# Attention scores by head pairs in a gated Flamingo layer with a mixture of experts, on one core

## What is computed

```python
def attn(ctx, latents, mask):               # latents = layernorm(x)
    xn, ln = layernorm(ctx), layernorm(latents)
    q  = ln @ Wq.T                          # 4 heads of 64
    kv = concat([xn @ Wkv.T, ln @ Wlkv.T])  # 64 + 1024 keys
    k, v = split(kv)
    qn, kn = rmsnorm(q) * SCALE, rmsnorm(k) # per head
    p = softmax(where(mask, qn @ kn.T, -max))
    return (p @ v) @ Wo.T + bo
x = x + tanh(g_xattn) * attn(ctx_768, layernorm(x), mask)
x = x + tanh(g_ffn) * top2_of_8_experts(layernorm(x))   # 256 -> 1024 -> 256
```

## Time and profile before

| | |
|---|---|
| runs, median | 1214.55 us (1213.91 to 1215.9, three runs) |
| profiled execution, span | 1218.7 us |
| PE busy | 1021.0 us (84%) |
| PEld busy | 828.1 us (68%) |
| DVE busy | 784.3 us (64%) |
| ACT busy | 688.7 us (57%) |
| POOL busy | 382.1 us (31%) |
| mean granted TensorE clock | 0.916 of full speed |

### The profile page before, as it was taken

One profiled execution on the slowest core, in us unless ns is written; L12 is line 12 of the kernel. 1 busy time (PEld: TensorE's weight loads), 2 busy tenths in 40 slices (PEclk: granted clock), 3 DMA queues, 4 the chain that ended last, 5 costly groups with the idle time before them and its releaser, 6 DMA issues. The chain is left out here.

```text
span 1218.7 us, 20071 instructions
## 1 busy us (share of the span) xinstructions
PE 1021.0 (84%) x5940; PEld 828.1 (68%) x5940; DVE 784.3 (64%) x1603; ACT 688.7 (57%) x1084; POOL 382.1 (31%) x275
## 2 busy tenths in 40 slices
PE   4689986699976798975898950799999999999992
PEld 4546565565665565654565650699999999999992
DVE  5946778666769565869574555366757575775751
ACT  4867758576848476848576811344544445463530
POOL 3510205316106234106242105134334343452321
PEclk9979999699989699999698975799999999999997
DMA  3010001101000100010110015324244242442325
GB/s 104 1 37 1 1 0 36 37 14 57 1 26 9 36 35 35 0 35 0 34 52 17 0 35 169 108 48 112 46 115 119 43 117 43 117 111 49 43 35 155
DMA packets 44964, 61.93 MB, mean 51 GB/s; under 512 B 7265, under 2 KB 38753, under 8 KB 44865
## 3 DMA queue, kind: packets, MB, share of 16 engines
q0 software_dynamic: 17520, 33.27, 12.2%
q1 hardware_dynamic: 27408, 28.29, 7.9%
HBM read 37.34 MB, written 28.39 MB: 54 GB/s over the span
## 5 line engine op out<-in xcount | busy, mean ns | idle before, releaser
L1500 PE MATMUL psH<-xT_hi,Q 128*128 128x256 f32 x1120 | 205.5, 282 | 10.8 <-DVE Q L1426 9.3
L1513 PE MATMUL psY<-K,g_hi 128*128 128x256 f32 x1120 | 203.3, 283 | 0.0
L1357 POOL DMA_INDIRECT total<-y_out,token_i x70 | 114.2, 1631 | 230.3 <-PE psH L1500 188.8
L1500 PEld LDWEIGHTS psH<-xT_hi,Q 128*128 128x128 f32 x1120 | 175.3, 190 | 12.5 <-issue 12.5
L1513 PEld LDWEIGHTS psY<-K,g_hi 128*128 128x128 f32 x1120 | 171.6, 188 | 0.0
L1500 PE MATMUL psH<-xT_lo,Q 128*128 128x256 f32 x560 | 157.6, 281 | 0.0
L1513 PE MATMUL psY<-K,g_lo 128*128 128x256 f32 x560 | 157.2, 281 | 0.0
L1390 ACT ACT_TABLE_LOAD x35 | 44.9, 1283 | 170.2 <-PE psH L1500 170.2
L1390 ACT ACTIVATE g<-psH,b_col 128x256 f32<-128x256 f32 x280 | 113.8, 473 | 30.6 <-DVE g_lo L1454 27.6
L630 ACT ACTIVATE p_ring_hi<-psS,shift 128x1024 fp32r<-128x1024 f32 x80 | 89.3, 1116 | 60.5 <-PE psS L1170 56.5
L472 POOL TENSOR_TENSOR rr<-ssm,minus_half 128x8 f32<-128x8 f32 (+1 forms) x36 | 60.0, 1666 | 194.5 <-DVE ssm L720 194.5
(11 more groups left out here) (226 smaller groups left out, 2182.9 us busy)
## 6 DMA issues: line engine op xcount, KB each, us to landing
lnf<-routed SPq DMA_DIRECT2D x35, 258.0 KB, 2.7
xr<-in_L_ffn_w POOLq DMA_DIRECT2D x7, 1024.0 KB
xn<-in_L_ffn_w POOLq DMA_DIRECT2D x7, 1024.0 KB
xr<-in_x SPq DMA_DIRECT2D x4, 1024.0 KB, 5.3
total<-xb SPq DMA_DIRECT2D x4, 1024.0 KB, 4.5
routed<-pad_rows SPq DMA_DIRECT2D x8, 258.0 KB
total<-y_out,token_i POOLq DMA_INDIRECT x70, 3.9
routed<-big,slot_i POOLq DMA_INDIRECT x64
```

Of the source, the lines that this page charges most:

```text
L1357: pool.indirect_dma_start(total, bass.IndirectOffsetOnAxis(ap=token_i[:, m:m + 1], axis=0), y_out[:, m, :], None, bounds_check=NTOK + TM - ...
L1500: ins = pe.matmul(o, l, r, start=(n == 0), stop=(n == len(parts) - 1))
L1513: ins = pe.matmul(psY[m][:, 0:D], l[:, c, cols], r[:, c, :], start=(c == 0 and n == 0), stop=(c == HC - 1 and n == 2))
```

## The change

A step of attention is no longer one head with 1024 queries but a pair of heads with 512 queries. Step index k = i // 9 now counts (pair, half of the queries); the 512 columns of the even head lie in the first PSUM bank of the buffer and those of the odd head in the second. The stacked tiles go: `q_hi`, `q_lo`, `k_hi`, `k_lo` hold each pair's even head on partitions 0 to 63 and its odd head on 64 to 127. The scores are three passes, each as two products of 64 rows, one on the lower row half and one on the upper. `heads_hi` has two instructions of 128 partitions for a tile, `heads_lo` two. V_lo of the context keys is read with all 128 rows (the upper 64 are zero). The denominators of a step now belong to two heads; their instructions keep their shapes. `attention_hi` waits for other counts, and for its last half pair it waits until all values are multiplied, since its target is one of the probability buffers. `attention_lo` of the first half stands ahead of the last denominators. The memset of K2's pad goes.

```diff
-            K2 = sb("K2", [P, H // 2, S + P], F32R)
...
+            PAIRS = H // 2
+            q_hi, q_lo = Q1[:, 0:PAIRS, :], Q1[:, PAIRS:H, :]
+            k_hi, k_lo = K1[:, 0:PAIRS, :], K1[:, PAIRS:H, :]
...
-                        for odd in range(2):
-                            keep, other = halves(odd)
-                            q_src, k_src, cols = turned_heads(t, keep)
-                            if t < T:
-                                act.activation(Q1[keep, odd:H:2, cols], q_src, ACT.Copy, scale=gqk[keep, 0:1])
-                            act.activation(K1[keep, odd:H:2, cols], k_src, ACT.Copy)
-                            ins = act.activation(K1[other, odd:H:2, cols], k_src, ACT.Copy)
-                        ins.then_inc(qk_hi_ready, 1)
+                        q_src, k_src, cols = turned_heads(t)
+                        if t < T:
+                            act.activation(q_hi[:, :, cols], q_src, ACT.Copy, scale=gqk[:, 0:1])
+                        act.activation(k_hi[:, :, cols], k_src, ACT.Copy).then_inc(qk_hi_ready, 1)
...
-                        act.wait_ge(o_read, b * 2 * H + (4 * c + 3 + n))
+                        act.wait_ge(o_read, b * 2 * H + (4 * c + 2 + 2 * n))
+                        if c == PAIRS - 1 and n == 0:
+                            act.wait_ge(av_done, b * NI + NI)
...
-                        for odd in range(2):
-                            keep, other = halves(odd)
-                            q_src, k_src, cols = turned_heads(t, keep)
-                            if t < T:
-                                dve.scalar_tensor_tensor(
-                                    out=Q1[other, odd:H:2, cols], in0=q_src, scalar=gqk[keep, 0:1],
-                                    in1=Q1[keep, odd:H:2, cols].bitcast(F32), op0=ALU.mult, op1=ALU.subtract)
-                            ins = dve.tensor_tensor(K2[keep, :, cols], k_src, K1[keep, odd:H:2, cols].bitcast(F32), ALU.subtract)
-                        ins.then_inc(qk_ready, 1)
+                        q_src, k_src, cols = turned_heads(t)
+                        if t < T:
+                            dve.scalar_tensor_tensor(out=q_lo[:, :, cols], in0=q_src, scalar=gqk[:, 0:1],
+                                                     in1=q_hi[:, :, cols].bitcast(F32), op0=ALU.mult, op1=ALU.subtract)
+                        dve.tensor_tensor(k_lo[:, :, cols], k_src, k_hi[:, :, cols].bitcast(F32), ALU.subtract).then_inc(qk_ready, 1)
...
                     denominators(H - 1, 0)
                     quotients(H - 1, 0)
+                    attention_lo(PAIRS - 1, 0)
                     denominators(H - 1, 1)
-                    attention_lo(H // 2 - 1, 0)
                     quotients(H - 1, 1)
-                    attention_lo(H // 2 - 1, 1)
+                    attention_lo(PAIRS - 1, 1)
...
-                        for n in range(2):
-                            pe.matmul(scores_psum(i)[:, n * HALF:(n + 1) * HALF], K1[:, h, keys], Q1[:, h, n * HALF:(n + 1) * HALF],
-                                      start=True, stop=False)
-                        rows_hi = slice(0, DH) if h % 2 == 0 else slice(DH, P)
-                        for n in range(2):
-                            ins = pe.matmul(scores_psum(i)[:, n * HALF:(n + 1) * HALF], K2[rows_hi, h // 2, keys],
-                                            Q1[rows_hi, h, n * HALF:(n + 1) * HALF], start=False, stop=True)
+                        keys, cols = slice(kt * P, (kt + 1) * P), slice(n * HALF, (n + 1) * HALF)
+                        products = ((k_hi, q_hi), (k_lo, q_hi), (k_hi, q_lo))
+                        for m, (kk, qq) in enumerate(products):
+                            for odd in range(2):
+                                rows_of = slice(odd * DH, (odd + 1) * DH)
+                                ins = pe.matmul(scores_psum(i)[:, odd * HALF:(odd + 1) * HALF], kk[rows_of, pair, keys],
+                                                qq[rows_of, pair, cols], start=(m == 0), stop=(m == len(products) - 1))
                         ins.then_inc(s_done, 1)
...
-                        vh, vl = V_hi[:, kt, v0:v0 + P], V_lo[0:p, kt, v0:v0 + P]
+                            vh, vl = V_hi[:, kt, v0:v0 + P], V_lo[:, kt, v0:v0 + P]
+                            products = [(vh, ph), (vh, pl), (vl, ph)] if kt < T else [(vh, ph), (vl, ph)]
```

More of the change, by code:

```diff
@@ new lines, in values @@
+                        ph, pl = p_hi[i % NP_RING], p_lo[i % NP_RING]
+                        for odd in range(2):
+                            v0 = (3 * (k // 2) + odd) * DH
+                            vh, vl = V_hi[:, kt, v0:v0 + P], V_lo[:, kt, v0:v0 + P]
+                            products = [(vh, ph), (vh, pl), (vl, ph)] if kt < T else [(vh, ph), (vl, ph)]
+                            cols = slice(odd * HALF, (odd + 1) * HALF)
+                            for m, (v, pr) in enumerate(products):
+                                ins = pe.matmul(psO[k % 2][:, cols], v, pr[:, cols], start=(kt == 0 and m == 0),
+                                                stop=(kt == KT - 1 and m == len(products) - 1))
```

77 lines of the change are left out of this document (34 added, 43 removed).

## The result

The changed kernel takes 1148.84 us (1147.09 to 1149.45, four runs), the kernel before beside it 1214.23 us (1212.41 to 1215.9): a ratio of 0.946, 95% interval 0.945 to 0.947. The profiled execution spans 1145.5 us, 73.2 less than the earlier trace rows.

A forecast was written before the change was run, and what follows sets the result against it. TensorE was taken to bound attention and VectorE the fronts. Attention 24.5 us (13.5, 8.3, 2.7) plus fronts 20 gave 44.5 off 1218.7, 1174.2; less 4.15, 1170 us, range 1155 to 1185 (chance 0.72), wider range 1155 to 1200.

The forecast's parts named there:

- The router's wait near the start of each later attention stays as it is: First steps of later attentions: the wait for the router was taken as unchanged, with no gain counted for it.
- the last line of the sum: Step from profiled span to median: 4.15 us taken off 1174.2, giving 1170 us.
- The 64-row stretch: Score products of an attention step: 0.97 us for three pairs, between load-bound 0.91 and 1.02; lower bound 0.88 side by side.
- Rival C: Better case: both halves' loads go in parallel (8 us), or VectorE's last scaling precedes GpSimd's addition; 1158 to 1162, within forecast range.
- The context keys' step: Attention step multiplying the 64 context keys: 2.10 us against 3.02, a gain of 0.92, nine times, 8.3 us.
- The four ends: Context-key products standing alone at the end of each attention: a gain of 0.68 us each, 2.7 in all.
- load-bound value: Score products with weight loads going one by one: 0.91 us at 0.10 a load, 1.02 at 0.12.
- The middle steps of later sequences: Steps 8 to 18 there: what they save is waited for at GpSimd's scatter chain, so no gain counted.
- The front's tile: VectorE's tile from 4.19 to 3.27 us in later sequences; first sequence 3.87 to 3.2, by a two-tile loop of 6.37.
- The end of the front: After the last tile's sums: GpSimd's addition holds VectorE's product for 5.54 us, so edits behind it gain nothing.
- Rival A: Score pairs run one after another: an ordinary step takes 3.17 us, the kernel is 16.5 slower, 1231; chance 0.15.
- Rival B: Pairs run together but ScalarE, GpSimd, VectorE or the front's loop absorb half the gain: 1192 us; chance 0.13.

The follow-up runs named there:

- e8: The kernel before, unchanged, profiled once more in one run: 1222.01 us, span 1220.1; on that chip the kernel before lies at 1223.41 us.
- e11: The kernel before with GpSimd's four subtractions at steps 19, 21, 28, 30 instead of 16, 18, 25, 27: 1220.36 us, ratio 0.994.
- e4: The changed kernel with GpSimd's four subtractions at steps 19, 21, 28, 30 instead of 16, 18, 25, 27, VectorE's norms moved with them: 1127.2 us, ratio 0.930.
- e1: The changed kernel with the score products reordered, the even head's three first, then the odd head's three: 1149.44 us.
- e7: The changed kernel with both heads' score products on the lower row half, so none run at once: 1237.71 us, ratio 1.010.
- e9: The changed kernel with GpSimd's addition held until the last heads are scaled and its four subtractions three steps later: 1101.25 us, ratio 0.899.
- e13: The changed kernel with all score products on one row half and GpSimd's addition held until the last heads are scaled: 1207.18 us, ratio 0.986.
- e14: The changed kernel with the front's heads on 64 partitions again, scores in pairs, and GpSimd's addition held until the last heads are scaled: 1138.59 us, ratio 0.931.
- e2: The changed kernel with the front's heads on 64 partitions again, four instructions each for heads_hi and heads_lo: 1169.67 us, ratio 0.963.
- e5: The changed kernel with GpSimd's addition of the residual held back until the last tile's heads are scaled: 1116.57 us, ratio 0.911.
- e3: The changed kernel with V_lo of the context keys read with 64 rows again: 1156.88 us, ratio 0.953.

## Why the prediction was wrong in size

The direction and the main cause were right: row halves run together, and without that the kernel would be slower than before. The step that failed is the one that put the first four steps of an attention at nothing, "The router's wait near the start of each later attention stays as it is": it is no wait but TensorE's own work below full clock, and it gave 15.1 us where 0.3 had been counted. That is half of the miss; the rest is in terms that were taken too small, and in the last line of the sum. By the table of stages: first steps 14.8, tiles of the front 5.2, steps 4 to 7 and 20 to 35 4.0, end of the front 3.6, steps 8 to 19 2.8, and the ends 1.6 the other way. On the profiled executions it was 1174.2 against 1145.5, 28.7 us; on the medians 1170 against 1148.84, 21.2. The difference of 7.5 is the step from span to median: I took off the 4.15 us by which the median lay under that one execution, but the changed kernel's median lies 3.3 above its profiled span. In every run whose span is on record the time is 1.5 to 1.9 us above it. So the profiled execution of the kernel before was some 6 us longer than the median one, and the changed kernel's was not, and such a surplus was no property to carry over. Where it lay is not shown; two places of the kernel before differ from one execution to the next by 2 and 4 us (e8).

**The 64-row stretch, taken at 0.97 us: too long.** It is 0.90, near the lower bound of 0.88. I had called the loads the part that goes one by one. In the rows they do, but both were loads of the same row half. On two halves they start 3 to 4 ns apart. Rival C named this and priced it at 8 us; in steps 4 to 7 and 20 to 35 it gave 4 of the 28.7. The bounds were right, and the choice between them went by a row that showed another case.

**The context keys' step, taken at 2.10: right but for the stretch.** It is 2.01, an ordinary step less two products as I had it, and it ties with ScalarE's two exponentials of the earlier trace rows. Some of it is given back: 0.46 us of waiting in the next step. The four ends, taken at 0.68 each, brought about 1 us together.

**The Trainium skill's rule on row groups**, in the page TensorE: Matmul & The Clock Gate, "The mechanism", was the better guide than my load-bound value. By its start distance of some 4 ns the stretch would be 0.88; the trace has 3 to 5 ns and 0.90.

**The middle steps of later sequences, counted as waited for: right.** From VectorE's slots to GpSimd's share of step 16 it is 24.1 us before (266.2 to 290.3) and 24.2 after (234.7 to 258.9). In the second sequence steps 8 to 19 gained 0.5 us of the 4.0 that their twelve steps save (33.3 us in e11 and 29.3 in e4, where no wait stands in them), with the wait up from 2.36 to 5.46 and its cost from 4.0 to 7.5, and e4 gave it back. The 5.0 us gained in the third and fourth sequences are mostly before's own late exponentials, which e11 shows to be something else; steps 8 to 15 are free of them in the changed kernel and in e1 to e7, but they come back in e9, so the change is no cure for them.

**The first steps, "the router's wait stays": the largest miss, 14.8 us.** I treated the start of a later attention as a wait with a fixed length. It is TensorE at work, busy for all of its 18.4 us, at a mean clock of 0.60. Steps 0 to 3 of the third sequence of the kernel before:
```profile
411.35:429.77 18.42, 18.42 (x61) 13.31 (x61) 5.46 (x10) 8.73 (x9) 0.00 (x0) 0.60 0.00 0
```
The same stretch of the changed kernel:
```profile
367.83:381.31 13.48, 13.48 (x69) 9.74 (x68) 5.24 (x10) 8.63 (x10) 0.00 (x0) 0.74 0.00 0
```
Length times clock gives the work at full clock: 11.0 us before and 9.9 after. At before's clock that saving of 1.1 is worth 1.9 us, and the rise from 0.60 to 0.74 the other 3.1. Over the four sequences the split is 6.7 and 8.3 us. With one execution each, and 2 us between executions of the kernel before in one sequence, the split is rough. The first share could have been worked out from the rows, had I put the clock beside the products; the second could not. e13 and e14 lay the clock on the pairs where no pause stands ahead; with the pause, as here, e2 gives the front a part of it. A row of the stage's clock is missing from the prediction.

**The front's tile, taken at 3.27 and 3.2: too long by 0.3.** It is 2.94 in all sequences, 5.2 us in sum. I took away the pair that goes, 0.92, and left the other instructions as they were. But the next ones are shorter too: the scaling holds 0.60 us and not 0.71 (L729 to L740, 187.35 to 187.95; 208.78 to 209.49 before), the remainders 0.40 and 0.33 and not 0.49 and 0.43. e2 still has the scaling at 0.60, so 0.11 of it does not hang on the number of instructions; in all 0.29 a tile does not. In the first sequence the loop over two tiles, which I had at 6.37, is at most 5.9: the overlap between its links was left out.

**The end of the front, "worth nothing": nearly.** In later fronts 0.56, 0.56 and 0.43 us, in the first 2.0. The reason was right, as e5 shows: without the hold the same edits are worth 3.1 us in each later front (8.49 less 5.39) and 3.9 in the first. The reading of the earlier trace rows was short by a link: the addition ends at 226.74 and the hold at 228.85, so the copy behind it holds VectorE too. The rule that I named there (SBUF — State Buffer, "Summary: rules for kernel authors" in the Trainium skill) agrees again for one instruction of GpSimd (4.71 us in the first front, where only the addition runs); that two in a row are waited out, 6.55 us, is what the later fronts show. It is 32 us of the kernel when the addition is moved out of the way.

Rival A's price was right to 0.01 us a step (e7), and its total of 16.5 us slower stands beside 14.3 in e7, in part by luck: the first steps lost 8 us there that it had not counted, and the fronts gained 5 more than it had. Rival B did not happen: its mechanism did, in steps 8 to 19, but it had been counted there. The range was too narrow at its low end because most gains were taken too small, and the two stretches that a faster kernel also changes, the clock and the tail of the front, stood at exactly nothing.

## What to carry to other kernels

Products of 64 rows on opposite row halves cost one product's time for two (0.23 us). So where three passes of 64 rows are due, pairing two heads beats stacking two of the passes on 128 rows and running the third with half the rows idle: three slots in place of four. A change between 64-row and 128-row products costs 0.19 us, so an operand padded to 128 rows can be the cheaper one (8.0 us in e3). Where a stretch runs below full clock, count its work at full clock and the clock as two terms, and put a range on the clock. After such a gain look at the engines that were hidden: here moving GpSimd's addition and its four subtractions gave 48 us more, beside the 65 of the change itself.

## What the runs showed of the hardware

- Two row halves are two streams with loads of their own: pairs start 3 ns apart (median of 432), and with the issue order grouped by half still only 10 ns apart, at no cost (e1). On one half six products take 1.58 us where three pairs take 0.90 (e7).
- VectorE's instructions of 256 elements a partition take 0.33 to 0.40 us from start to start on 128 partitions (after), 0.39 to 0.46 on one half after the other (e2) and 0.43 to 0.51 where every other one reads one half and writes the other (before), though each handles the same elements a partition. Of the 1.18 us saved in a tile e2 lays 0.89 on their number and width; 0.29 remain.
- A VectorE product that started behind GpSimd's addition ended 0.28 us after the addition where nothing followed it, and 0.28 us after GpSimd's next instruction, a copy, where one did (before and after, all fronts).
- TensorE comes back at half clock from a wait of 5.46 us, which makes that wait cost 7.5 (e4), and a wait of 2.36 costs 4.0 (before, e11). The first four steps of a later attention run at a mean clock of 0.85 with paired products and of 0.64 to 0.79 without, after the same front (e5, e13).
